# Gated cross-attention and low-rank FFN on one core: a new order of the start-up, identity products on TensorE, and stacks that alternate by batch

## What is computed

```python
def _L0_xattn_ref(h, v):
    p = jax.nn.softmax(jnp.einsum('bsd,bvd->bsv', h, v), axis=-1)
    return jnp.einsum('bsv,bvd->bsd', p, v)
def _L0_ffn_ref(h, W, b, lora_down, lora_up, down_aux, up_aux):
    lilora_weight = up_aux @ (lora_up @ (lora_down @ down_aux))
    return jnp.einsum('bsi,oi->bso', h, W) + b + jnp.einsum('bsi,oi->bso', h, lilora_weight)
x = x + jnp.tanh(g_xattn[0]) * _L0_xattn_ref(_layernorm(x), ctx)
x = x + jnp.tanh(g_ffn[0]) * _L0_ffn_ref(_layernorm(x), W, b, lora_down, lora_up, down_aux, up_aux)
```

## Time and profile before

| what | value |
|---|---|
| median of 3 executions | 319.59 us (319.36 to 319.92) |
| the profiled execution | 316.71 us, of which the span from first to last instruction is 314.9 us |
| TensorE (PE) busy | 299.9 us, 95% of the span |
| VectorE (DVE), ScalarE (ACT), GpSimd (POOL) busy | 234.6, 187.0, 221.3 us |
| DMA | 60.60 MB moved, mean 192 GB/s |

### The profile page before, as it was taken

One profiled execution on the slowest core, in us unless ns is written; L12 is line 12 of the kernel. 1 busy time (PEld: TensorE's weight loads), 2 busy tenths in 40 slices (PEclk: granted clock), 3 DMA queues, 4 the chain that ended last, 5 costly groups with the idle time before them and its releaser, 6 DMA issues.

```text
span 314.9 us, 6478 instructions
## 1 busy us (share of the span) xinstructions
PE 299.9 (95%) x2072; PEld 283.3 (90%) x2072; DVE 234.6 (75%) x745; ACT 187.0 (59%) x546; POOL 221.3 (70%) x271
## 2 busy tenths in 40 slices
PE   4788999999999999999999999999999999999991
PEld 0668999998999999999899999999899999999981
DVE  3685778797588877798497778788587778777864
ACT  1674665656476565666466566656476665656651
POOL 3136777777577778777577877778488777887752
PEclk9999999999999999999999999999999999999998
DMA  7947254455398655555199765555198955443112
GB/s 218 412 184 192 91 191 166 176 202 203 126 262 263 221 193 200 200 202 203 65 260 288 233 223 200 202 185 180 39 285 282 275 203 201 166 177 127 67 46 89
DMA packets 17755, 60.60 MB, mean 192 GB/s; under 512 B 2360, under 2 KB 2360, under 8 KB 17722
## 3 DMA queue, kind: packets, MB, share of 16 engines
q1 hardware_dynamic: 17074, 59.26, 55.8%
q10 hardware_dynamic: 648, 0.95, 0.9%
HBM read 35.84 MB, written 16.78 MB: 167 GB/s over the span
## 4 chain that ended last, share of the span: by engine, by line
PE 90%; DMA 3%; ACT 1%; DVE 1%; SPq 1%; POOL 1%; issue 1%; POOLq 0%; DVEq 0%; ACTq 0%
PE y_ps L481 64%; PE y_ps L509 9%; PE a_ps L504 9%; PE c_ps L471 3%; DMA w_rows<-in_w 2%; PE y_ps L489 2%; DMA stacks<-v_lo 1%; SPq L220 1%; PE a_ps L471 1%; PE y_ps L539 1%; PE y_ps L548 1%; DVE o_sb L654 0%; ACT w_cent L412 0%; DVE x L616 0%; POOL x_bias L292 0%
## 5 line engine op out<-in xcount | busy, mean ns | idle before, releaser
L481 PE MATMUL y_ps<-wc,xT 128*128 128x334 f32 (+1 forms) x1536 | 228.1, 302 | 0.0
L481 PEld LDWEIGHTS y_ps<-wc,xT 128*128 128x128 f32 x1536 | 214.3, 189 | 2.0
L292 POOL TENSOR_TENSOR x_bias<-x,bias_g 128x512 f32<-128x512 f32 x63 | 81.1, 1288 | 65.4 <-DVE x L616 65.4
L280 POOL TENSOR_TENSOR xT<-xt_raw,xT 128x512 fp32r<-128x512 f32 x64 | 83.3, 1301 | 9.5 <-ACT xT L357 9.5
L372 ACT ACTIVATE expd<-y_ps,neg_max,rs 128x77 f32<-128x77 f32 x64 | 26.6, 416 | 81.9 <-DVE neg_max L606 81.9
L386 ACT ACTIVATE squares<-x,x_nmean 128x512 f32<-128x512 f32 x64 | 46.4, 725 | 18.7 <-DVE x_nmean L624 18.7
L303 POOL TENSOR_TENSOR rs<-stat_eps,half_neg 128x2 f32<-128x2 f32 (+1 forms) x67 | 46.1, 688 | 5.2
L654 DVE SCALAR_TENSOR_TENSOR o_sb<-y_ps,rs,x_bias 128x512 f32<-128x512 f32 x64 | 48.0, 751 | 1.6 <-POOL rs L303 1.6
L509 PEld LDWEIGHTS y_ps<-stacks,pT 109*128 109x128 f32 (+1 forms) x256 | 39.8, 191 | 5.4
L637 DVE TENSOR_TENSOR pT<-y_ps,pT 13x128 fp32r<-13x128 f32 x64 | 18.6, 290 | 34.9 <-ACT pT L363 34.9
L616 DVE SCALAR_TENSOR_TENSOR x<-a_ps,x_sb 128x512 f32<-128x512 f32 x64 | 43.7, 683 | 1.2 <-PE a_ps L504 1.2
(11 more groups left out here) (64 smaller groups left out, 181.1 us busy)
## 6 DMA issues: line engine op xcount, KB each, us to landing
xt_raw<-in_xt SPq DMA_DIRECT2D x32, 512.0 KB, 6.0
x_sb<-in_x SPq DMA_DIRECT2D x32, 512.0 KB, 5.0
out<-o_sb SPq DMA_DIRECT2D x31, 512.0 KB, 3.3
stacks<-v_hi SPq DMA_DIRECT2D x8, 308.0 KB
stacks<-v_hi SPq DMA_DIRECT2D x8, 256.0 KB
stacks<-v_lo SPq DMA_DIRECT2D x8, 256.0 KB
w_rows<-in_w ACTq DMA_DIRECT2D x1, 512.0 KB, 4.7
w_rows<-in_w SPq DMA_DIRECT2D x1, 512.0 KB, 7.6
```

The lines of the kernel that those rows point to most:

```text
L280: pool.tensor_tensor(xT[:, k % TRING, 1, :, :], xt_raw[:, k % XRING // UNIT, k % UNIT, :, :], xT[:, k % TRING, 0, :, :].bitcast(F32), ALU. ...
L292: pool.tensor_tensor(x1_bias[:, q, :], x1[:, j, :], bias_g[:, :], ALU.add).then_inc(x1b_ready, 1)
L481: mm = pe.matmul(y_half(k, h)[:, 0:n], xT[:, k % TRING, part, c, :], wc[:, c, w, h * H:h * H + n], start=(c == 0 and part == 0 and w == 0) ...
```

## The change

- **W in four loads.** `load_w` takes one chunk of 128 rows (256 KB) instead of two; SP issues chunks 0 and 1, ScalarE's queue 2 and 3. The context rows are now first in ScalarE's queue, low_out second, xt unit 0 last. SP waits for chunk 3 of W before it issues x unit 0 and the bias, waits for x unit 0, then issues units 1 and 2, the hi part of the stacks, and unit 3.
- **Low-rank parts.** The mean and centring of the first product move from VectorE to ScalarE; the second product goes into a bank of y_ps instead of c_ps. The centring of W chunk 3 moves to GpSimd.
- **Context of batch 0.** VectorE takes its statistics and centring first of all; its transposes stand between the low-rank products in TensorE's queue; ScalarE and VectorE split it before wc; GpSimd copies its columns into wc. VectorE takes row_stats(0) before ctx_rows_lo(0).
- **Identity products.** TensorE multiplies the identity by itself into an unused part of y_ps, 12, 4, 6, 4 and 4 times, at five places of the start-up.
- **W transposes.** Output chunks 0 and 1 as before; chunks 2 and 3 are interleaved with the low-rank products, input chunk by input chunk.
- **Stacks.** One set for each batch, in `stacks[:, n % 2]`, issued before unit 6; SP issues the three hi DMAs, and the two lo DMAs come after them, in batch 0 from ScalarE's queue.

```diff
+        def load_w(eng, c):
+            eng.dma_start(w_rows[:, c, :], W[c * P:(c + 1) * P, :]).then_inc(ld_w[c], 16)
+
+        def stack_lo(eng, n):
+            eng.wait_ge(v_lo_ok, 2 * n + 2)
+            lo, to = v_lo[:, :].bitcast(F32), stacks[:, n % 2, :, :].bitcast(F32)
+            for rows, source in ((to[V:V + R, 0, :], lo[Q:V, :]), (to[Q:P, 1, :], lo[0:Q, :])):
+                eng.dma_start(rows, source).then_inc(stacked[n % 2], 16)
...
+            def stack_hi(n):
+                if n < 2:
                     sp.wait_ge(zeroed, 1)
                 else:
-                    sp.wait_ge(y_ready, TB * n - (HB if part == 0 else 0))
+                    sp.wait_ge(y_ready, TB * (n - 1))
                 sp.wait_ge(v_hi_ok, 2 * n + 2)
...
             sp.dma_start(low_in_sb[:, :], low_in).then_inc(ld_in, 16)
-            sp.dma_start(low_out_sb[:, :], low_out).then_inc(ld_out, 16)
+            load_w(sp, 0)
             load_w(sp, 1)
-            load_xt(0, 0)
+            sp.wait_ge(ld_w[KC - 1], 16)
             load_x(0, 0)
-            for u in range(1, XRING // UNIT):
+            sp.dma_start(b_row[:, 0:D], b_gates[0:D].partition_broadcast(P)).then_inc(ld_b, 16)
+            sp.wait_ge(ld_x[0], 16)
+            for u in range(1, 3):
                 load_xt(u, u)
                 load_x(u, u)
-            for part in range(2):
-                stack_rows(0, part)
+            stack_hi(0)
+            load_xt(3, 3)
+            load_x(3, 3)
...
-                    if k >= NU - 2:
-                        stack_rows(n + 1, k - (NU - 2))
+                    if k == NU - 2:
+                        stack_hi(n + 1)
+                        stack_lo(sp, n + 1)
...
+            def first_columns():
+                pool.wait_ge(ct_lo_ok, 1)
+                for part in range(2):
+                    pool.tensor_copy(wc[:, :, part, D:D + V], ct[:, part, :, :].bitcast(F32)).then_inc(c_cols, 1)
...
+                if t == -2:
+                    first_columns()
...
+            pool.wait_ge(w_nmean_ok, 2)
+            pool.tensor_scalar(w_cent[:, 3, :], w_rows[:, 3, :], w_nmean[:, 1:2], None, ALU.add)\
+                .then_inc(w_centred[3], 1)
...
-            load_w(act, 0)
             act.dma_start(c_rows[:, :], ctx_in[0]).then_inc(ld_ctx, 16)
+            act.dma_start(low_out_sb[:, :], low_out).then_inc(ld_out, 16)
+            load_w(act, 2)
+            load_w(act, 3)
             act.dma_start(b_row[:, D:D + 2], b_gates[D:D + 2].partition_broadcast(P)).then_inc(ld_gates, 16)
-            act.dma_start(b_row[:, 0:D], b_gates[0:D].partition_broadcast(P)).then_inc(ld_b, 16)
+            act.dma_start(xt_raw[:, 0:1, :, :, :].rearrange("p o n c r -> p (o n c r)"),
+                          xt_in[0:1].rearrange("o p e -> p (o e)")).then_inc(ld_xt[0], 16)
...
+            act.wait_ge(low_mm, 1)
+            act.activation(squares[0:LR, :], a_ps[0:LR, :], ACT.Copy, scale=-1.0 / D,
+                           accum_out=dn_nmean[:, :]).then_inc(dn_nmean_ok, 1)
+            act.wait_ge(dn_nmean_ok, 1)
+            act.activation(dn_st[:, :], a_ps[0:LR, :], ACT.Identity, bias=dn_nmean[:, :]).then_inc(dn_hi_ok, 1)
+
+            for i in range(2):
+                act.wait_ge(ld_w[2 + i], 16)
+                act.activation(w_cent[:, 2 + i, :], w_rows[:, 2 + i, :], ACT.Copy, scale=-1.0 / D,
+                               accum_out=w_nmean[:, i:i + 1]).then_inc(w_nmean_ok, 1)
+
+            act.wait_ge(low_mm, 2)
+            act.activation(up_st[:, :], up_bank(), ACT.Copy).then_inc(up_hi_ok, 1)
+            act.wait_ge(w_nmean_ok, 1)
+            act.activation(w_cent[:, 2, :], w_rows[:, 2, :], ACT.Identity, bias=w_nmean[:, 0:1])\
+                .then_inc(w_centred[2], 1)
+            prep(0, TURN)
             act.wait_ge(ld_gates, 16)
             act.activation(tg[:, :], b_row[:, D:D + 2], ACT.Tanh).then_inc(tg_ok, 1)
...
+            x_hi(0, 0)
...
                 act.activation(wc[:, c, 0, 0:D], w_bank(c), ACT.Copy, scale=tg[:, 1:2]).then_inc(w_hi_ok, 1)
-                if c == 0:
-                    prep(0, TURN)
             ctx_rows_hi(0)
-            ctx_columns(0)
+            x_hi(1, 1)
             ctx_product_hi(0)
+            act.wait_ge(zeroed, 1)
+            stack_lo(act, 0)
             act.wait_ge(ld_b, 16)
             act.activation(bias_g[:, :], b_row[:, 0:D], ACT.Copy, scale=tg[:, 1:2]).then_inc(biasg_ok, 1)
...
+            def stay_busy(count):
+                for _ in range(count):
+                    pe.matmul(y_ps[:, 0, 1, 0:P], ident[:, :], ident[:, :], start=True, stop=True)
+
+            pe.wait_ge(ident_ok, 4)
+            stay_busy(12)
             pe.wait_ge(ld_in, 16)
...
-                pair = k % TB // HB
-                if k % HB == 0:
-                    pe.wait_ge(stacked[pair], 16 * DMAS * (t // TB + 1))
+                pair = t // TB % 2
+                if k % TB == 0:
+                    pe.wait_ge(stacked[pair], 16 * DMAS * (t // TB // 2 + 1))
...
+            stay_busy(4)
+            prep(0, TURN)
+            pe.wait_ge(ld_out, 16)
+            pe.matmul(up_bank(), low_out_sb[:, 0:LR], low_out_sb[:, LR:LR + D], start=True, stop=True)\
+                .then_inc(low_mm, 1)
+            stay_busy(6)
+            for o in range(2):
+                pe.wait_ge(w_centred[o], 1)
+                for c in range(KC):
+                    w_transpose(o, c)
+                stay_busy(4)
             for c in range(KC):
+                for o in range(2, KC):
+                    if c == 0:
+                        pe.wait_ge(w_centred[o], 1)
+                    w_transpose(o, c)
+                if c == 0:
+                    pe.wait_ge(dn_ok, 1)
+                    pe.wait_ge(up_ok, 1)
                 pe.matmul(w_bank(c), dn_st[:, c * P:(c + 1) * P], up_st[:, :], start=False, stop=True,
                           skip_group_check=True).then_inc(w_tr, 1)
-            prep(0, TURN)
             prep(0, PRODUCT)
...
+            prep(0, STATS)
+            dve.wait_ge(c_own, 1)
+            ctx_mean(0)
+            prep(0, CENTRE)
+
             for c in range(2):
+                dve.wait_ge(ld_w[c], 16)
                 dve.bn_stats(w_bn[:, c, :], w_rows[:, c, :]).then_inc(w_own, 1)
...
+            dve.wait_ge(dn_hi_ok, 1)
...
+            prep(0, TURN)
...
+            row_stats(0, 0)
             ctx_rows_lo(0)
-            row_stats(0, 0)
             prep(0, TAKE)
```

More of the change, by code:

```diff
@@ L64, in build_kernel @@
         dn_st = sb("dn_st", [LR, D], F32R)
-        dn_bn = sb("dn_bn", [LR, 6])
-        dn_mv = sb("dn_mv", [LR, 2])
+        dn_nmean = sb("dn_nmean", [LR, 1])
         w_rows = sb("w_rows", [P, KC, D])
@@ L132, in cw_ps, with up_bank @@
             return a_ps[0:V, :] if n == 0 else c_ps[0:V, :]
+        def up_bank():
+            return y_ps[0:LR, 0, 0, :]
         def w_bank(c):
@@ L139, in build_kernel @@
         st_o = [sem(f"st_o{i}") for i in range(ORING // UNIT)]
-        ld_w = [sem(f"ld_w{i}") for i in range(2)]
+        ld_w = [sem(f"ld_w{i}") for i in range(KC)]
         ld_b, ld_gates, ld_in, ld_out, ld_ctx = (sem(n) for n in ("ld_b", "ld_gates", "ld_in", "ld_out", "ld_ctx"))
         zeroed, ident_ok, tg_ok, biasg_ok = (sem(n) for n in ("zeroed", "ident_ok", "tg_ok", "biasg_ok"))
-        low_mm, dn_own, dn_ok, up_hi_ok, up_ok = (sem(n) for n in ("low_mm", "dn_own", "dn_ok", "up_hi_ok", "up_ok"))
-        w_centred = [sem(f"w_centred{i}") for i in range(2)]
+        low_mm, dn_nmean_ok, dn_hi_ok, dn_ok, up_hi_ok, up_ok = (
+            sem(n) for n in ("low_mm", "dn_nmean_ok", "dn_hi_ok", "dn_ok", "up_hi_ok", "up_ok"))
+        w_centred = [sem(f"w_centred{i}") for i in range(KC)]
         w_own, w_nmean_ok, w_tr, w_hi_ok, w_lo_ok = (sem(n) for n in ("w_own", "w_nmean_ok", "w_tr", "w_hi_ok", "w_lo_ok"))
@@ L209, in load_ctx @@
                 sp.dma_start(c_rows[:, :], ctx_in[n:n + 1].rearrange("o v d -> (o v) d")).then_inc(ld_ctx, 16)
-            def stack_rows(n, part):
-                if n == 0:
+            def stack_hi(n):
+                if n < 2:
                     sp.wait_ge(zeroed, 1)
                 else:
-                    sp.wait_ge(y_ready, TB * n - (HB if part == 0 else 0))
+                    sp.wait_ge(y_ready, TB * (n - 1))
                 sp.wait_ge(v_hi_ok, 2 * n + 2)
-                hi, lo, to = v_hi[:, :].bitcast(F32), v_lo[:, :].bitcast(F32), stacks[:, part, :, :].bitcast(F32)
+                hi, to = v_hi[:, :].bitcast(F32), stacks[:, n % 2, :, :].bitcast(F32)
                 for rows, source in ((to[0:V, 0, :], hi), (to[96:K0, 0, :], hi[Q:V, :]), (to[0:Q, 1, :], hi[0:Q, :])):
[L220 to L223, removed]
+                    sp.dma_start(rows, source).then_inc(stacked[n % 2], 16)
             def unit(u):
@@ L326, in ctx_rows_hi @@
                 else:
-                    for s in stacked:
-                        act.wait_ge(s, 16 * DMAS * n)
```

(29 more changed lines are left out.)

16 lines of the change are left out of this document (1 added, 15 removed).

## The result

The changed kernel takes 316.30 us in the median (315.63 to 317.04, 12 executions); the kernel before took 319.38 (317.43 to 319.92, 12 executions). The ratio is 0.991 (95% interval 0.9887 to 0.9932): 3.1 us faster. The prediction said 318.3 and a range from 316.6; the direction was right, the size 2.4 times too small and the median just outside.

What follows compares the result with a forecast made beforehand. TensorE bounds the kernel, so only tile 0's p_product start counts: 1.1 us earlier plus 0.24 of restart gives 1.3. 316.71 - 1.3 + 2.88 = 318.3 us, range 316.6 to 321.0.

Steps and rivals of the forecast that it cites:

- The base: Starting time of the sum: the profiled execution's 316.71 us, with 2.88 us added to reach the median of 319.59.
- Rival C: Timed executions' extra 2.88 us lies partly in W's landing, so the gain is 2 to 3 us; chance 0.12.
- The clock in the list: TensorE's start-up: identity products raise the clock within its 19.75 us list, ending at 13.8; nothing won here.
- 11.5 + s/2: End of TensorE's start-up list in us; s, time from its start until the clock rises, was taken as 4.6.
- Rival A: At start-up the clock doesn't rise during the identity products: 321.0 to 322.0 us, up to 325.9; chance 0.15.
- W: Start-up loads of W in four: landed by 9.12 us at worst, just covered by TensorE's list; 256 KB estimated at 2.6.
- The hole in wc: ScalarE's wait for the context transposes between wc chunks goes, as the context copy is done before: 0.9 us won.
- exponents(0) behind the DMA issues: Tile 0's softmax: ScalarE's two low DMA issues and bias_g delay exponents(0) to 22.3 us, eating the gain before it.
- stacks: Batch 0's copies before p_product: last landing at 25.1 us, between 24.3 and 25.97, so the wait for them goes.
- the restart: Tile 0's p_product: TensorE arrives without a stop, so 4.57 us becomes the steady 4.33, 0.24 us won.
- Rival B: Before p_product the transfers into stacks still end last: a gain of 0.2 us, 319.4 us; chance 0.08.
- Batches 1 to 3: Tile loop: one stacks set instead of two per batch, with 8 us of cover before and after: 0 us.

Runs made afterwards that it cites:

- e15: The kernel before, unchanged, run again for a third trace; ratio 0.9990 to the kernel before.
- e1: The kernel before, unchanged, run again for a second trace; ratio 0.9986 to the kernel before.
- e5: The changed kernel, unchanged, run again as a reference; ratio 0.9918 to the kernel before.
- e2: The kernel before with 12 identity products added at the start and nothing else; ratio 0.9958 to the kernel before.
- e13: The changed kernel without identity products and with batch 0's two lo DMAs issued by SP; 315.47 us, ratio 0.9892 to the kernel before.
- e8: The changed kernel with 12, 4, 3, 1, 1 identity products instead of 12, 4, 6, 4, 4; ratio 0.9881 to the kernel before.
- e6: The kernel before with 12 identity products at the start and 8 between the halves of the W transposes; ratio 0.9904 to the kernel before.
- e10: The changed kernel with 12, 4, 3, 1, 1 identity products and batch 0's lo DMAs issued by SP; 314.66 us, ratio 0.9854 to the kernel before.
- e7: The changed kernel with the loads of x unit 3 issued before the hi part of the stacks; ratio 0.9951 to the kernel before.
- e3: The changed kernel without its identity products; 316.93 us in the median of four executions, ratio 0.9883 to the kernel before.

## Why the prediction missed

**The base.** The sum took the profiled execution's own time and added 2.88 us to get to the median, as if these were a constant beside it. For the most part they were low clock in the very stretch that the change works on: p_product starts 2.35 and 3.0 us later in e15 and e1, of which 0.24 and 0.65 are W's landing, and by median spans (314.9 against 317.0) it is 2.1 us. Rival C had the right form (the usual execution of before is slower at the start, and the new one is proof against it) with the wrong cause, W's landing, and a chance of 0.12. The base is the step of the prediction that failed. A sum from a typical execution, p_product at 29.4 to 30.0 against 26.1 to 27.2, gives 2.2 to 4.0 us.

**The clock in the list.** Held. The prediction's end of the list, 11.5 + s/2, gives 13.3 with the 3.6 us at the low level that e5's 24 instructions in 4.50 us show, and 14.4 with the 5.8 in the changed kernel's trace (5.49 for the 24, and a little of L473); the first L582 started at 13.28 and 14.43. The row that frightened (5.8 us of work without a rise) stands in each trace of before, but not with identity products at the start: they had the clock up by 7.4 us in all nine traces that begin with them. Rival A did not occur.

**W.** Held: its four chunks landed at 6.05, 7.49, 7.70 and 8.26, before the old 9.12. They took 4.9 to 6.2 us from issue to landing among the other loads, so the 2.6 us estimated for 256 KB did not apply here; the cover was enough all the same.

**The hole in wc.** Held: ScalarE's four chunks run in 2.42 us from 15.01 without a stop, and the context product ends 4.4 us after their start, where the chain of the earlier trace rows needed 5.4.

**exponents(0) behind the DMA issues.** Right in kind, short in size: 23.16, where 22.3 plus 0.6 for the longer s was expected. The two issues took 1.52, bias_g followed, and TensorE waited 1.4 us for the probabilities.

**stacks.** Wrong. Between 3.40 us after the last issue and the whole 6.57 again I took the middle, on the thought that two queues are faster. They took 6.91 from the first issue to the last landing, above the upper bound, and the last to land was a copy of v_hi. So a wait for stacks was left, 0.3 us, and with it the 0.24 us of the restart (31.82 - 27.23 = 4.59, the steady tile 4.33). The late softmax counts beside it: TensorE had its x_product done at 26.9, where the sum has 25.95 plus 0.6 for the longer s. In this trace, with s at 5.8, the sum had 0.7 us of gain and the trace shows a loss of 0.2; the 0.9 between them is some 0.4 of softmax, 0.3 of copies and 0.24 of restart. Rival B, 0.08, names this wait. So there were two errors of opposite sign: 2.4 to 3.0 us too little for the base, 0.9 too much for the sum. The right direction owes something to luck: between the two profiled executions nothing was gained, and e5's trace (p_product at 26.07) gains 1.0 us on the early one; the rest came from the base, which the sum did not have.

**Batches 1 to 3.** Held: 0 us, by the constant 287.9.

## What to carry to other kernels

Before a change is costed at the start of a kernel, see whether the profiled execution is a typical one: if its time lies below the timed ones, the difference has a place, and here it was in the stretch at issue. A wait can cost twice, once as time and once in the matmuls after it, as after the 2.1 us in e2 and the 2.4 us in e13; fill or remove the wait, and do not add work where none is left. A start-up chain is worth what its last link lets through: in e8 1.4 us won ahead of the stacks' copies brought 0.2 at p_product.

## What the runs showed that I had not expected

- A wait of 2.13 us (e2, in eight of ten executions by their mean clock) and one of 2.37 us (e13) each were followed by the 1.2 GHz level; waits of 1.0 to 1.6 us with the clock up (e6, e10, e8, e7) were not.
- The granted-clock column reads 1.00 from the start on, also while spacings show the low level (e1 up to 22 us); it shows a fall only once the clock has been up (e2, e13). For the start, spacings have to be read.
- Splitting the five copies into stacks (924 KB) over two queues brought nothing: v_hi to p_product 6.8 to 6.9 us from one queue (but 8.2 in e13), 6.9 to 8.3 from two. What made 8 us of it in e3, e8 and e13 is open.
- GpSimd took 1.57 us to add a column to 128x512, more than the 1.30 of its two-input form in the earlier trace rows, which I had taken as the upper bound; it was covered:

```profile
10.85 1.57 POOL L330 TENSOR_SCALAR w_cent<-w_rows,w_nmean 128x512 f32<-128x512 f32 x1 [7.53 <-ACT w_cent L436]
```
